# A mixed-expert 3x3 convolution on one core: a finer start, another order of the first pairs, and the last pair in row groups of 8, 8, 7 and 5

## What is computed

```python
pooled = x.mean(axis=(2, 3))          # of the normalised x
a = relu(pooled @ fc1_w.T + fc1_b)
att = softmax(a @ fc2_w.T + fc2_b)
agg_w = einsum('bk,koihw->boihw', att, weight)
agg_b = att @ bias
out = x + conv3x3(group_norm(x), agg_w) + agg_b
```

## Time and profile before

| | us |
|---|---|
| median of 3 runs | 309.3 (309.04 to 309.43) |
| the profiled execution | 309.06 |
| its span, first to last instruction | 307.2 |
| TensorE (PE) busy | 299.5, 97% |
| VectorE (DVE) busy | 244.4, 80% |
| ScalarE (ACT) busy | 186.8, 61% |
| GpSimd (POOL) busy | 22.9, 7% |
| mean granted TensorE clock | 0.997 of full |

### The profile page before, as it was taken

How to read it: one execution, slowest core, us unless ns; L and a number is a source line. 1 busy time by engine, 2 the same in 40 slices (tenths; PEclk the granted TensorE clock), 3 DMA queues, 4 the chain that set the end, 5 groups by cost and what they waited for, 6 DMA issues and landing times.

```text
span 307.2 us, 15832 instructions
## 1 busy us (share of the span) xinstructions
PE 299.5 (97%) x7068; PEld 263.8 (86%) x7068; DVE 244.4 (80%) x763; ACT 186.8 (61%) x238; POOL 22.9 (7%) x32
## 2 busy tenths in 40 slices
PE   8799999999999999999999999999999999999994
PEld 6667879697777997767788998899999999999994
DVE  4998997979999999888898989878796978856000
ACT  1484918376292838558296868667684866768321
POOL 1013040400400000000000000000000000000000
PEclk9999999999999999999999999999999999999998
DMA  6992957748375576757646767684857242332333
GB/s 211 341 413 83 227 150 193 234 110 247 110 212 135 174 191 197 191 169 212 186 133 152 258 174 242 170 253 119 241 134 227 96 133 70 109 99 83 92 106 106
DMA packets 31012, 53.62 MB, mean 175 GB/s; under 512 B 6752, under 2 KB 23264, under 8 KB 30944
## 3 DMA queue, kind: packets, MB, share of 16 engines
q1 hardware_dynamic: 30720, 52.49, 58.1%
q10 hardware_dynamic: 224, 0.12, 0.2%
HBM read 26.89 MB, written 25.69 MB: 171 GB/s over the span
## 4 chain that ended last, share of the span: by engine, by line
PE 91%; DVE 5%; DMA 1%; ACT 1%; issue 0%; DVEq 0%
PE acc L801 91%; DVE stats L322 1%; DMA x<-x 1%; DVE mix L437 1%; DVE wparts L341 0%; PE tiny L770 0%; ACT xh L629 0%; ACT wh L646 0%; DVE o L601 0%; DVE mix L435 0%; DVE mix L443 0%; ACT mix L665 0%; DVE logit L405 0%; DVE mv L330 0%; DVE prod L402 0%
## 5 line engine op out<-in xcount | busy, mean ns | idle before, releaser
L801 PE MATMUL acc<-xh,wh 64*64 64x385 f16 (+3 forms) x2304 | 111.2, 325 | 0.8 <-ACT wh L646 0.3
L801 PE MATMUL acc<-xl,wh 64*64 64x385 f16 (+3 forms) x2304 | 110.6, 325 | 0.1
L801 PE MATMUL acc<-xh,wl 64*64 64x385 f16 (+3 forms) x2304 | 110.3, 325 | 0.0
L801 PEld LDWEIGHTS acc<-xl,wh 64*64 64x64 f16 x2304 | 88.8, 107 | 9.8 <-issue 1.4
L801 PEld LDWEIGHTS acc<-xh,wh 64*64 64x64 f16 x2304 | 86.7, 107 | 12.1 <-ACT wh L659 1.8
L801 PEld LDWEIGHTS acc<-xh,wl 64*64 64x64 f16 x2304 | 86.5, 107 | 11.2
L684 ACT ACTIVATE o<-acc,par 128x392 f32<-128x392 f32 x64 | 42.8, 669 | 54.1 <-PE acc L801 54.1
L322 DVE BATCH_NORM_STATS2 stats<-x 128x6 f32<-128x448 f32 x112 | 64.9, 615 | 3.7 <-DMA x<-x 3.7
L637 ACT ACTIVATE xh<-x,xof,xsc 128x1568 f16<-128x1568 f32 x24 | 40.5, 1690 | 31.4 <-DVE xof L396 31.4
L508 DVE TENSOR_TENSOR xl<-x,xh 128x1568 f16<-128x1568 f32 x28 | 49.9, 1786 | 8.6 <-ACT x L611 8.5
L437 DVE SCALAR_TENSOR_TENSOR mix<-w_sb,ex,mix 128x192 f32<-128x192 f32 (+1 forms) x72 | 44.1, 612 | 0.5
(11 more groups left out here) (62 smaller groups left out, 139.7 us busy)
## 6 DMA issues: line engine op xcount, KB each, us to landing
x<-x SPq DMA_DIRECT2D x48, 392.0 KB, 4.0
out<-o SPq DMA_DIRECT2D x64, 196.0 KB, 3.4
out<-o SPq DMA_DIRECT2D x127, 98.0 KB, 2.7
x<-x SPq DMA_DIRECT2D x6, 784.0 KB, 10.2
x<-x SPq DMA_DIRECT2D x3, 448.0 KB, 4.4
w_sb<-w_t SPq DMA_DIRECT2D x2, 288.0 KB, 2.9
w_sb<-w_t SPq DMA_DIRECT2D x1, 576.0 KB, 5.3
crossed<-par SPq DMA_DIRECT2D x32, 0.5 KB, 2.7
```

Source lines behind the costliest of these rows:

```text
L801: ins = nc.tensor.matmul(pixels[:, top:bottom, left:right], weights[i][halves[m], tap * C:(tap + 1) * C], window, start=start and step == ...
```

## The change

- Pair 0 is loaded in seven pieces of one chunk, each with its own semaphore; the weights are issued after the fifth.
- In pair 0 ACT makes xh in eight strips of 392 pixels (`high_strip`), in the order 1, 4, 2, 5, 3, 6, 0, 7, and TensorE waits for the strips a set needs. The first quarter of x is rescaled by DVE (`normalise_first_quarter`) and not by ACT.
- In pairs 1 to 3 TensorE's sets go (part 0 and part 1 of groups 0 and 1, then of group 2, then part 2). DVE makes xh's last quarter between the second and the third part of the mixture, and rescales x ahead of the low weights. ACT evicts both halves of the old pair's last group ahead of the third weight part.
- In pairs 0 to 3 POOL makes the lower half of xl in two operations (840 and 728 pixels); TensorE's groups 0 and 1 wait for the first only.
- Pair 4's wh comes in two operations, the middle row first; TensorE starts on it with three taps. In pairs 4 to 6 ACT evicts group 1 ahead of the next wh.
- In pair 8 groups go two by two: xh products of both, then xl products of both. `SUMS_AT` moves for pairs 4, 5 and 8.
- The last pair's regions are cut into groups of 8, 8, 7 and 5 rows (`band`).

The diff, cut to its core (renamed uses of `band` and of the semaphores are left out):

```diff
+SPLIT = HALF + 2 * GN + W
+LAST_ROWS = (8, 8, 7, 5)
...
-PIECES = ((0, 2), (2, 4), (4, 6), (6, 7))
...
+FIRST_STRIPS = (1, 4, 2, 6)
...
-SUMS_AT = ((1, 2, 3), (1, 2, 2), (1, 2, 2), (1, 2, 2), (1, 0, 6), (1, 0, 0), (0, 2, 6), (0, 2, 4), (0, 1, 2))
+SUMS_AT = ((1, 2, 3), (1, 2, 2), (1, 2, 2), (1, 2, 2), (1, 0, 8), (1, 0, 1), (0, 2, 6), (0, 2, 4), (1, 0, 2))
...
-               ((0, 0), (0, 1), (1, 0), (1, 1), (2, 0), (2, 1), (0, 2), (1, 2), (2, 2)))
+               ((0, 0), (0, 1), (1, 0), (1, 1), (0, 2), (1, 2), (2, 0), (2, 1), (2, 2)))
...
+def band(p, g, r):
+    rows = LAST_ROWS if p == PAIRS - 1 else GROUPS * (ROWS,)
+    at = sum(rows[:g])
+    if r == 0:
+        row = rows[-1] + at if g < GROUPS - 1 else 0
+    else:
+        row = REGION + at
+    return row, rows[g], at * W
...
-            for n, (first, last) in enumerate(PIECES):
-                pixels = slice(first * CHUNK, last * CHUNK)
-                sp.dma_start(x_sb[0][:, pixels], x_d[0, :, pixels]).then_inc(x_piece[n], 16)
-            sp.wait_ge(x_piece[2], 16)
+                    sp.dma_start(*lower_rows(p, m, g)).then_inc(stored[i][1], 16)
+            for n in range(CHUNKS):
+                pixels = slice(n * CHUNK, (n + 1) * CHUNK)
+                sp.dma_start(x_sb[0][:, pixels], x_d[0, :, pixels]).then_inc(x_chunk[n], 16)
+            sp.wait_ge(x_chunk[4], 16)
...
-                nc.gpsimd.tensor_tensor(rows_of(xl[i], 1), rows_of(x_sb[p], 1), rows_of(xh[i], 1),
-                                        ALU.subtract).then_inc(s_xl[1], 1)
+                for start, end, done in ((HALF, SPLIT, s_xl_first), (SPLIT, PIX, s_xl[1])):
+                    nc.gpsimd.tensor_tensor(xl[i][:, start:end], x_sb[p][:, start:end], xh[i][:, start:end],
+                                            ALU.subtract).then_inc(done, 1)
...
+            def last_quarter(p):
+                i = p % 2
+                dve.wait_ge(s_norm, p + 1)
+                if p >= 2:
+                    dve.wait_ge(s_conv, 2 * GROUPS * (p - 1))
+                pixels = slice(3 * HALF // 2, PIX)
+                nc.vector.tensor_scalar(xh[i][:, pixels], x_sb[p][:, pixels], xsc[i][:], xof[i][:], ALU.mult,
+                                        ALU.add).then_inc(s_quarter[3], 1)
             def mixture_in_parts(p):
                 dve.wait_ge(s_exp, p + 1)
                 if p >= 1:
                     dve.wait_ge(s_wh, mixed(p - 1))
                 for n, part in enumerate(PARTS):
+                    if p >= 1 and n == 2:
+                        last_quarter(p)
...
+            def normalise_first_quarter():
+                dve.wait_ge(s_quarter[0], 1)
+                v = x_sb[0][:, 0:HALF // 2]
+                nc.vector.tensor_scalar(v, v, xsc[0][:], xof[0][:], ALU.mult, ALU.add).then_inc(s_scaled, 1)
...
+            normalise_first_quarter()
             low_weights(0)
             weights_bound()
+            dve.wait_ge(s_scaled, 1)
...
                 mixture_in_parts(p)
-                last_quarter(p)
+                normalise(p, 0)
                 low_weights(p)
-                normalise(p, 0)
                 low_inputs(p, 0)
...
+            def high_strip(n):
+                act.wait_ge(s_norm, 1)
+                pixels = slice(n * GN, (n + 1) * GN)
+                ins = nc.scalar.activation(xh[0][:, pixels], x_sb[0][:, pixels], ACT.Identity,
+                                           bias=xof[0][:], scale=xsc[0][:])
+                if n in FIRST_STRIPS:
+                    ins.then_inc(s_strip, 1)
+                else:
+                    ins.then_inc(s_quarter[n // 2], 1)
...
-                nc.scalar.activation(wh[i][:], mix[:], ACT.Copy, scale=wsc[i][:]).then_inc(s_wh, 1)
+                high, mixed_w = (t.rearrange("p (r n) -> p r n", r=3) for t in (wh[i], mix))
+                for rows in (slice(1, 2), slice(0, 3, 2)) if p == EARLY else (slice(0, 3),):
+                    nc.scalar.activation(high[:, rows], mixed_w[:, rows], ACT.Copy, scale=wsc[i][:]).then_inc(s_wh, 1)
...
-            high_quarter(0, 0)
+            high_strip(1)
             exponentials(0)
-            high_quarter(0, 2)
+            high_strip(4)
             first_share(1)
-            high_quarter(0, 1)
+            high_strip(2)
+            high_strip(5)
+            high_strip(3)
             high_weights_part(0, 0)
             first_share(2)
-            high_quarter(0, 3)
+            high_strip(6)
+            high_strip(0)
             high_weights_part(0, 1)
-            normalise_quarter(0, 0)
+            high_strip(7)
             high_weights_part(0, 2)
...
-                results(p - 1, 3, (0,))
+                results(p - 1, 3)
                 high_weights_part(p, 2)
-                results(p - 1, 3, (1,))
...
+                        results(p, 1)
                         high_weights(p + 1)
-                        results(p, 1)
                         results(p, 2)
...
+                    if p == 0:
+                        if (n, g) == (0, 0):
+                            pe.wait_ge(s_strip, 2)
+                        elif (n, g) == (0, 1):
+                            pe.wait_ge(s_strip, 3)
+                            pe.wait_ge(s_quarter[2], 1)
+                        elif (n, g) == (0, 2):
+                            pe.wait_ge(s_quarter[1], 1)
+                            pe.wait_ge(s_strip, 4)
+                        elif (n, g) == (1, 0):
+                            pe.wait_ge(s_quarter[0], 1)
+                        elif (n, g) == (2, 0):
+                            pe.wait_ge(s_quarter[3], 1)
...
-                    pe.wait_ge(s_wh, mixed(p))
+                    pe.wait_ge(s_wh, max(mixed(p) - 1, mixed(p - 1) + 1))
                     for half in range(2):
                         high_inputs_made(pe, p, half)
                     for g in range(SLOTS):
                         slot_free(p, g)
-                        high(p, g)
+                        if (p, g) == (EARLY, 0):
+                            high(p, g, range(3))
+                            pe.wait_ge(s_wh, mixed(p))
+                            high(p, g, range(3, TAPS))
+                        else:
+                            high(p, g)
...
-                for half in range(2):
-                    pe.wait_ge(s_xl[half], p + 1)
+                pe.wait_ge(s_xl[0], p + 1)
+                pe.wait_ge(*((s_xl_first, p + 1) if p < EARLY else (s_xl[1], p + 1)))
                 for g in range(SLOTS):
+                    if g == 2:
+                        pe.wait_ge(s_xl[1], p + 1)
                     low(p, g, 1)
...
+            p = GROUPED
+            pe.wait_ge(s_wh, mixed(p))
+            for half in range(2):
+                high_inputs_made(pe, p, half)
+            for first in range(0, GROUPS, 2):
+                for g in (first, first + 1):
+                    slot_free(p, g)
+                    high(p, g)
+                    pe.wait_ge(s_wl, p + 1)
+                    low(p, g, 0)
+                for g in (first, first + 1):
+                    for half in range(2):
+                        pe.wait_ge(s_xl[half], p + 1)
+                    low(p, g, 1)
+            for p in range(GROUPED + 1, PAIRS):
```

More of the change, by code:

```diff
@@ L152, in dynamic_conv @@
         s_wpart = sem("s_wpart")
-        x_piece = [sem(f"x_piece{n}") for n in range(len(PIECES))]
+        x_chunk = [sem(f"x_chunk{n}") for n in range(CHUNKS)]
         x_in = [sem(f"x_in{i}") for i in range(X_RING)]
@@ L315, in chunk_stats @@
                     if p == 0:
-                        for n, (first, last) in enumerate(PIECES):
-                            if t == first:
-                                dve.wait_ge(x_piece[n], 16)
+                        dve.wait_ge(x_chunk[t], 16)
                     elif t == start:
```

55 lines of the change are left out of this document (25 added, 30 removed).

## The result

| | before | changed |
|---|---|---|
| median, us | 309.24 | 308.62 |
| lowest to highest, 8 runs each | 308.98 to 309.43 | 308.14 to 309.44 |
| profiled execution | 309.06 | 308.6 |
| its span | 307.2 | 306.8 |

What follows compares the result with a forecast made beforehand. TensorE, busy 299.5 of 307.2 us, was taken as the bound, so only its stops counted. Gains of 1.06 + 0.17 + 0.16 - 0.12 + 0.35 = 1.62 us gave 307.6 us (chance 0.64), range 306.6 to 308.6.

Steps and rivals of the forecast that it cites:

- The step that failed: Load of pair 0: with seven pieces, the seventh statistics start at 7.5 instead of 7.81, 0.3 us sooner.
- Strips: Pair 0: ACT's strips take 0.59 us each from start to start; with earlier data, the steady stream still begins 0.12 later.
- Pairs 1 to 3: TensorE's holes close, but DVE's chain to the sums limits the gain to 0.30, 0.38 and 0.38, sum 1.06 us.
- the closest distance seen: Pairs 1 to 3: least time from sums ready to sums read, 0.18 us, added to DVE's chain.
- Pair 4: TensorE starts 0.32 us earlier after a smaller wh copy, then waits 0.15 before the second group: gain 0.17.
- Pair 8 and the last pair: Pair 8: half of a 0.33 us hole gained, 0.16; last pair: shorter eviction and stores after the last group, 0.35.
- rival 3: Last pair: a floor under the short steps costs 0.9 us more, time 308.5; chance 0.05.
- Rival 1: DVE and ACT hold everything back in pairs 1 to 3, strips cost 0.65: gain 0.6, time 308.7 us; chance 0.13.
- Rival 4: Pairs 1 to 3: ACT's eviction delays the third weight copy; at 1.1 us delay, slower, 310.5; chance 0.04.
- Rival 2: All holes close in full and the prologue gains 0.3: gain 2.65, time 306.7 us; chance 0.14.
- Rival 5: The change does nothing: finer load pieces land no sooner and strips cost as bounded; no chance of its own.
- case 1's price: The cost in Rival 1, gain 0.6 and time 308.7 us, said to include finer pieces landing no sooner.

Runs made afterwards that it cites:

- e1: The changed kernel with pair 0 loaded in the four old pieces (2, 2, 2, 1 chunks); 307.83 us, ratio 0.9961.
- e3: The changed kernel with pair 0 loaded in four pieces of 1, 2, 2, 2 chunks; 308.62 us, ratio 0.9985.
- f2: The changed kernel with pair 0 loaded in six pieces of 2, 1, 1, 1, 1, 1 chunks; 308.24 us, ratio 0.9965.
- e4: The changed kernel with pair 0's four old load pieces and ACT's quarters in place of strips; 307.38 us, ratio 0.9943.
- g2: e4 with the old order of pairs 1 to 3 (TensorE's sets, DVE's quarter and rescaling, ACT's eviction); 307.91 us, ratio 0.9962.
- g3: e4 with POOL's lower half of xl in one operation again; 307.69 us, ratio 0.9952.
- f4: e4 with the last pair in four groups of 7 rows again; 307.75 us, ratio 0.9948.

## Why the prediction was wrong, step by step

- **The step that failed: "the first piece lands at 3.95 ... the data hold it at 7.3, or later for the three extra issues and smaller packets (no row shows that; up to 0.5 later). I take 7.5: 0.3 sooner; bounds 0 and 0.5."** The first came even sooner (3.31), but the third came at 6.54, where my sum has it at 3.95 + 2 x 0.56 = 5.07, and the statistics ended 1.01 later, not 0.3 sooner. The rest of the kernel passed this delay on to pair 1's start. I took the rate of a queue full of large loads (224 KB in 0.56 us) for a queue that begins with small ones, and gave the unknown cost a bound only in the direction of a gain. e1, e3 and f2 show that it was a first piece of one chunk that brought the gap. This one term is 1.3 of the 1.42 us that the start was off; the middle's surplus hid a part of it.
- **Strips: right in kind, a little small.** Forecast 0.59 from start to start, measured (1.91 - 0.70) / 2 = 0.605. From the exponential to the first copy I had 2.90, it was 16.82 - 13.86 = 2.96. The start lost 1.54 - 1.01 = 0.53 beside the statistics, against my 0.42, and e4 without them gains about 0.5. By the cycle table of the Trainium skill ("VectorE: DVE Perf Modes", section The TRN2 errata) a strip would be an estimated 0.51; the measured 0.605 decides, while its advice against small tiles holds here.
- **Pairs 1 to 3: right in kind, too small: "DVE wins: the gain is 0.30, not 0.39".** TensorE got its holes back in full: 1.39, by single pairs 0.43, 0.47 and 0.49, where I had 1.06. I had shortened DVE's chain by 0.10. In the changed kernel pair 2's sums are ready (DVE in order of time)

```profile
47.37 0.15 DVE L417 TENSOR_TENSOR sums<-std,wbound 128x1 f32<-128x1 f32 x1
```
at 47.52, 17.32 after the reading at 30.20, where it was 17.59; and they are read at 47.86, 0.34 later, so DVE had 0.16 to spare over the closest distance seen. The chain got 0.27 shorter, not 0.10. The rescaling gave 0.12 of it, as counted (1.13 to the next start before, 1.01 now). Another 0.12 I had not counted came from the moved quarter: before, the third part's first operation started 0.45 behind the start of the second part's last (33.52, 33.97); now the quarter starts 0.33 behind it (35.06, 35.39). g2 and g3 take the two holes back one at a time.
- **Pair 4: 0.07 for 0.17.** The start came 0.21 nearer where I had 0.32, since DVE's mixture came late; the hole before group 2 took back 0.14 of it (forecast 0.15).
- **Pair 8 and the last pair: right in kind.** The 0.20 for 0.16 is partly luck: pair 8 itself takes 178.26 - 160.45 = 17.81 where it took 178.46 - 160.37 = 18.09, so it gained 0.28, and 0.08 went again behind it, which is not explained. The end has 0.28 for 0.35, and f4 against e4 has 0.37. There is no floor under the short steps (0.112 a step, and 18.16 for the last pair with either cut): rival 3 is refuted.
- **Rival 1** named a time near the measured one (308.7) for a reason that didn't occur: DVE did not hold the cycle, and strips did not cost 0.65. **Rival 4**, the slower one, needed the third copy to be late; it ended 0.31 before its reader.
- **Rival 2** had the middle right, with all holes closing (1.35; it was 1.39), and the start wrong in the same step as the forecast.
- **Rival 5** said that finer pieces might land no sooner, and I put it "inside case 1's price". The real case was worse than its bound. The range's upper end should have taken in a start 1 us later: 307.6 + 1.1 = 308.7 would have held the result.

## What to carry to other kernels

Don't take the landing time of a cut-up load from the rate of the large ones: look at the trace for the rate after the first pieces, or keep the first piece as it was and cut only those behind. A term that no row shows needs a bound on the side of a loss as well, above all at the start, where nothing lies beside it. And a change of many parts is best tried part by part: here the parts that reordered the middle gave more than they promised, and leaving out two parts of the start makes it three times the gain.
